# A gated cross-attention and feed-forward block on one core: the first layer of the feed-forward stage as seven half-sized block products

## The reference

```python
x = x + tanh(g_xattn) * attention(layernorm(x), ctx, ctx, w_q, w_k, w_v)   # causal, 8 x 1024 rows of 512
h = gelu(einsum('bsd,fd->bsf', layernorm(x), ternary(W1)) + b1)             # 512 -> 2048, exact gelu
x = x + tanh(g_ffn) * (einsum('bsf,df->bsd', h, ternary(W2)) + b2)          # 2048 -> 512
```

## Time and profile before

| | |
|---|---|
| median of 3 runs | 1661.05 us |
| profiled execution, own time | 1659.3 us |
| its span | 1657.5 us |
| TensorE busy (8492 products) | 1625.6 us, 98% |
| VectorE, ScalarE, GpSimd busy | 54%, 39%, 19% |
| TensorE clock granted, mean | 0.994 |
| feed-forward stage: its first second-layer product | at 769.41 us |
| one group of 512 rows in that stage | (1652.5 - 823.1) / 15 = 55.3 us |

### The profile page before, as it was taken

One profiled execution on the slowest core, in us unless ns is written; L12 is line 12 of the kernel. 1 busy time (PEld: TensorE's weight loads), 2 busy tenths in 40 slices (PEclk: granted clock), 3 DMA queues, 4 the chain that ended last, 5 costly groups with the idle time before them and its releaser, 6 DMA issues.

```text
span 1657.5 us, 23707 instructions
## 1 busy us (share of the span) xinstructions
PE 1625.6 (98%) x8492; PEld 830.7 (50%) x8492; DVE 889.5 (54%) x1595; ACT 652.3 (39%) x1032; POOL 311.5 (19%) x337
## 2 busy tenths in 40 slices
PE   7899999999999999999999999999999999999998
PEld 4455655565655565554444444444444444444444
DVE  6656666575666568884344344434443444344432
ACT  2333333333243345333443444434443544344443
POOL 3211111111111111131122112211221122122200
PEclk9899999999999999999999999999999999999999
DMA  6446455545545489953122212221222022202210
GB/s 203 113 97 148 103 143 106 139 106 132 120 98 148 92 237 224 214 139 102 44 52 70 63 36 59 70 63 26 69 70 63 19 76 70 63 19 76 70 32 26
DMA packets 261398, 157.50 MB, mean 95 GB/s; under 512 B 222080, under 2 KB 222096, under 8 KB 260048
## 3 DMA queue, kind: packets, MB, share of 16 engines
q1 hardware_dynamic: 260432, 154.21, 36.4%
q10 hardware_dynamic: 720, 2.10, 0.3%
q0 software_dynamic: 176, 0.27, 0.1%
HBM read 70.53 MB, written 33.55 MB: 63 GB/s over the span
## 4 chain that ended last, share of the span: by engine, by line
PE 89%; DVE 3%; issue 2%; DMA 1%; ACT 1%; SPq 0%; POOL 0%; DVEq 0%; ACTq 0%
PE s_ps L1090 12%; PE e_ps L1090 12%; PE s_ps L1016 11%; PE o_ps L1048 11%; PE t_ps L978 10%; PE v_ps L997 10%; PE o_ps L952 6%; PE t_ps L952 6%; PE v_ps L952 6%; PE m_ps L952 6%; DVE v_s L890 1%; DMA raw<-out_y 1%; DVE v_s L916 0%; ACT v_s L563 0%; ACT g L560 0%
## 5 line engine op out<-in xcount | busy, mean ns | idle before, releaser
L890 DVE SCALAR_TENSOR_TENSOR v_s<-g,sc,v_s 128x512 f16<-128x512 f32 x256 | 245.6, 969 | 382.4 <-ACT v_s L563 377.1
L1090 PE MATMUL s_ps<-w_s,v_s 128*128 128x512 f16 x1024 | 262.9, 379 | 6.2 <-DVE v_s L890 6.1
L1090 PE MATMUL e_ps<-w_s,v_s 128*128 128x512 f16 x1024 | 262.8, 379 | 0.0
L1016 PE MATMUL s_ps<-ctx_s,tT 128*128 128x512 f16 (+3 forms) x1152 | 199.3, 328 | 2.3 <-DVE tT L727 2.3
L1048 PE MATMUL o_ps<-v_s,pT 128*128 128x512 f16 x840 | 191.6, 379 | 0.0
L481 ACT ACTIVATE p<-s_ps,ebias,esc 128x128 f32<-128x128 f32 (+3 forms) x64 | 53.2, 831 | 351.3 <-DVE ebias L769 351.3
L563 ACT ACTIVATE v_s<-g,sc 128x512 f16<-128x512 f32 x256 | 184.8, 722 | 8.4
L978 PE MATMUL t_ps<-xnT,a_s 128*128 128x256 f16 x1488 | 175.9, 276 | 8.8 <-issue 8.7
L997 PE MATMUL v_ps<-wv_s,ctx_s 128*128 128x512 f16 x768 | 177.9, 382 | 2.8 <-DVE v_s L734 2.8
L1090 PEld LDWEIGHTS s_ps<-w_s,v_s 128*128 128x128 f16 x1024 | 98.9, 98 | 130.4 <-DVE v_s L890 10.8
L978 PEld LDWEIGHTS t_ps<-xnT,a_s 128*128 128x128 f16 x1488 | 146.0, 99 | 33.4 <-issue 10.4
(11 more groups left out here) (127 smaller groups left out, 1599.6 us busy)
## 6 DMA issues: line engine op xcount, KB each, us to landing
x_ring<-in_x SPq DMA_DIRECT2D x64, 256.0 KB, 2.9
out_y<-x_ring SPq DMA_DIRECT2D x64, 256.0 KB, 2.1
raw<-out_y SPq DMA_DIRECT2D x64, 256.0 KB, 3.1
out_y<-v_s SPq DMA_DIRECT2D x64, 256.0 KB, 2.1
raw<-in_ctxT SPq DMA_DIRECT2D x7, 2048.0 KB, 8.7
w_in<-in_w1T SPq DMA_DIRECT2D x16, 512.0 KB, 4.2
w_in<-in_w2T SPq DMA_DIRECT2D x16, 512.0 KB, 4.9
raw<-in_ctxT SPq DMA_DIRECT2D x2, 1024.0 KB, 16.8
```

Source lines behind the costliest of these rows:

```text
L890: v.scalar_tensor_tensor(out=g_s[:, f % 4, LO], in0=g32[:, f % 2], scalar=col(C_SG), in1=g_s[:, f % 4, HI], op0=ALU.mult, op1=ALU.subtract ...
L1016: last_mm = mm(s_ps[:, lo:hi], tT[:, pr, ta, c, q * P:(q + 1) * P], ctx_s[:, par, ca, c, lo:hi], start=(n == 0 and c == 0), stop=(n == 2 a ...
L1090: last_mm = mm(y_ps[i], g_s[:, f % 4, a, i * P:(i + 1) * P], w2_s[:, f, :], start=(f == 0 and a == HI), stop=(f == FC - 1 and a == LO))
```

## The change

Each group's first layer is written as 2 x 2 blocks: the 512 rows in two halves of 256, the inner dimension in two halves of 256, the hidden units in pairs of 128. Seven block products (Strassen's scheme in the form with 15 additions) take the place of eight. A unit `U` is 4 blocks `f` of one group, so there are 64 units. In each unit:

- TensorE: `unit_product` 1 to 7, each 8 products of 128 weights x 256 rows (56 instead of 32 products of 512), in four pieces (`unit_first`, `_second`, `_third`, `_last`) that alternate with the four blocks of the second layer (`back`) of the unit before.
- Three PSUM banks are copied out by ScalarE (R1, R2, R3) and one by VectorE (R5); two sums are made on VectorE and one on GpSimd (`last_sum`); gelu runs on 8 pieces of 256 columns, six of them from SBUF.
- The normalized rows are made in pairs of tiles (`y_stats`, `y_scale`, `y_normal`): four sums of 256 columns on GpSimd (`y_sums`), then one upper-half pass of 1792 columns on ScalarE (`y_upper`), one lower-half pass of 1792 columns on GpSimd (`y_lower`), and one DMA transpose of 3584 columns (`turn_y`). There are two pairs to a group.
- Weight sums: four sums of 1024 columns on GpSimd and four on VectorE, once, in the last slots of the attention stage.
- The feed-forward loops are written out; before, they were loops of the sequencers.

```diff
+            def turn_y(q):
+                sp.wait_ge(y_lo, q + 1)
+                dst = yT[q // 2 % 2].rearrange("p a o c n -> p (a o c) n")[:, :, q % 2 * P:(q % 2 + 1) * P]
+                sp.dma_start_transpose(dst, rows_at(q)[1].rearrange("p a o n -> p (a o n)")).then_inc(y_turned, 16)
...
+            def y_sums(q):
+                r8 = rows_at(q)[0]
+                pool.wait_ge(y_rows, 2 * q + 2)
+                g.tensor_tensor(r8[:, 4], r8[:, 0], r8[:, 2], ALU.subtract).then_inc(y_comb, 1)
+                g.tensor_tensor(r8[:, 6], r8[:, 1], r8[:, 0], ALU.subtract).then_inc(y_comb, 1)
+                pool.wait_ge(y_comb, 4 * q + 1)
+                g.tensor_tensor(r8[:, 5], r8[:, 1], r8[:, 4], ALU.subtract).then_inc(y_comb, 1)
+                pool.wait_ge(y_comb, 4 * q + 3)
+                g.tensor_tensor(r8[:, 7], r8[:, 3], r8[:, 5], ALU.subtract).then_inc(y_comb, 1)
...
+            def y_lower(q):
+                r8, r7 = rows_at(q)
+                pool.wait_ge(y_hi, q + 1)
+                g.tensor_tensor(r7[:, LO].rearrange("p o n -> p (o n)"), r8[:, 1:8].rearrange("p o n -> p (o n)"),
+                                r7[:, HI].rearrange("p o n -> p (o n)"), ALU.subtract).then_inc(y_lo, 1)
...
+            def weight_sums():
+                pool.wait_ge(w_ternary, NW // 2)
+                pool.wait_ge(t_mm, NT)
+                for c in range(2):
+                    g.tensor_tensor(wS[0][:, c], w1v[:, 0, c, :, 1], w1v[:, 1, c, :, 1], ALU.add).then_inc(w1_sums, 1)
+                for c in range(2):
+                    pool.wait_ge(w1_sums, c + 1)
+                    g.tensor_tensor(wS[1][:, c], wS[0][:, c], w1v[:, 0, c, :, 0], ALU.subtract).then_inc(w1_sums, 1)
...
+            def last_sum(U):
+                pool.wait_ge(r5_out, U + 1)
+                pool.wait_ge(r3_out, U + 1)
+                g.tensor_tensor(rr[:, R3], rr[:, R3], rr[:, R5], ALU.add).then_inc(c22_sum, 1)
...
+            last_sum(0)
+            for U in range(NU):
+                G = U // UG + 1
+                if U % UG == 0 and G < NG:
+                    y_scale(G * GT)
+                    y_scale(G * GT + 1)
+                if U % UG == 1 and G < NG:
+                    y_scale(G * GT + 2)
+                    y_scale(G * GT + 3)
+                    y_lower(2 * G)
+                    y_sums(2 * G + 1)
+                if U % UG == 2 and G < NG:
+                    y_lower(2 * G + 1)
+                    for e in range(GT):
+                        add_bias(G * GT + e)
+                if U + 1 < NU:
+                    last_sum(U + 1)
+                if U % UG == 0 and G < NG:
+                    y_sums(2 * G)
...
+            def unit_top(U, rows_q=None, rows_q_late=None):
+                act.wait_ge(h_mm[1], U + 1)
+                a.activation(rr[:, R1], bank_a[U % 2], ACT.Copy).then_inc(r1_out, 1)
+                if rows_q is not None:
+                    y_upper(rows_q)
+                act.wait_ge(c11_sum, U + 1)
+                if U:
+                    act.wait_ge(g_split, 4 * U - 2)
+                for p in range(2):
+                    gelu(U, p, 2 * p, 0, halves(rr[:, R1], p))
+                act.wait_ge(h_mm[6], U + 1)
+                a.activation(rr[:, R2], bank_a[U % 2], ACT.Copy).then_inc(r2_out, 1)
+                act.wait_ge(c12_sum, U + 1)
+                for p in range(2):
+                    gelu(U, 2 + p, 2 * p, 1, halves(rr[:, R2], p))
+                upper(U, 0, 3)
+                act.wait_ge(h_mm[7], U + 1)
+                a.activation(rr[:, R3], bank_a[U % 2], ACT.Copy).then_inc(r3_out, 1)
+                upper(U, 1, 4)
+                if rows_q_late is not None:
+                    y_upper(rows_q_late)
+            def unit_end(U):
+                act.wait_ge(c22_sum, U + 1)
+                if U:
+                    act.wait_ge(g_split, 4 * U)
+                for p in range(2):
+                    gelu(U, 4 + p, 2 * p + 1, 1, halves(rr[:, R3], p))
+                act.wait_ge(h_mm[4], U + 1)
+                for p in range(2):
+                    gelu(U, 6 + p, 2 * p + 1, 0, halves(bank_a[U % 2], p))
+                act.wait_ge(g_act, 8 * U + 8)
+                act.sem_inc(c21_read, 1)
+                upper(U, 2, 7)
+                upper(U, 3, 8)
...
+            def y_normal(e):
+                r, u = e % 2, e // GT % 2 * GT + TILE[e % GT]
+                slots = (2, 4) if r == 0 else (0, 2)
+                dst = rows_at(e // 2)[0][:, slots[0]:slots[1]].rearrange("p o n -> p (o n)")
+                dve.wait_ge(y_rstd, e + 1)
+                if e >= 2:
+                    dve.wait_ge(y_lo, e // 2)
+                v.tensor_scalar(dst, x2_in[:, u], mv[:, r, 0:1], rstd[:, r:r + 1], ALU.subtract,
+                                ALU.mult).then_inc(y_rows, 1)
...
+            def unit_first(U):
+                dve.wait_ge(h_mm[5], U + 1)
+                if U:
+                    dve.wait_ge(c22_sum, U)
+                v.tensor_copy(rr[:, R5], bank_c).then_inc(r5_out, 1)
+                dve.wait_ge(h_mm[2], U + 1)
+                dve.wait_ge(r1_out, U + 1)
+                v.tensor_tensor(rr[:, R1], rr[:, R1], bank_b, ALU.add).then_inc(c11_sum, 1)
+            def unit_second(U):
+                dve.wait_ge(h_mm[3], U + 1)
+                dve.wait_ge(r2_out, U + 1)
+                v.tensor_tensor(rr[:, R2], rr[:, R2], bank_c, ALU.add).then_inc(c12_sum, 1)
...
+            lower(0, 0)
+            lower(0, 1)
+            for U in range(NU):
+                G = U // UG + 1
+                if U and U % UG == 0:
+                    finish_rows(U // UG - 1)
+                if U + 1 < NU:
+                    unit_first(U + 1)
+                lower(U, 2)
+                lower(U, 3)
+                if U % UG == 1 and G < NG:
+                    for e in (G * GT + 2, G * GT + 3):
+                        y_stats(e)
+                    for e in (G * GT + 2, G * GT + 3):
+                        y_normal(e)
+                if U + 1 < NU:
+                    unit_second(U + 1)
+                    lower(U + 1, 0)
+                    lower(U + 1, 1)
+                if U % UG == 0 and G < NG:
+                    for e in (G * GT, G * GT + 1):
+                        y_stats(e)
+                    for e in (G * GT, G * GT + 1):
+                        y_normal(e)
+            finish_rows(NG - 1)
...
+            def unit_product(U, k, first):
+                g, bank = U // UG, (bank_a[U % 2], bank_b, bank_c)[(0, 0, 1, 2, 0, 2, 0, 0)[k]]
+                row = (None, B11, B21, B22, T4, T1, T2, T3)[k]
+                for p in range(2):
+                    m = U % UG * 2 + p
+                    for a in (HI, LO):
+                        for c in range(2):
+                            w = (None, w1v[:, 0, c, m, 0], w1v[:, 1, c, m, 0], wS[3][:, c, m], w1v[:, 1, c, m, 1],
+                                 wS[0][:, c, m], wS[1][:, c, m], wS[2][:, c, m])[k]
+                            last_mm = mm(bank[:, p * 2 * P:(p + 1) * 2 * P], w, yT[g % 2][:, a, row, c, :],
+                                         start=(first and p == 0 and a == HI and c == 0),
+                                         stop=(a == LO and c == 1), skip_group_check=True)
+                last_mm.then_inc(h_mm[k], 1)
...
+            def unit_first(U):
+                if U % UG == 0:
+                    pe.wait_ge(y_turned, 16 * (2 * (U // UG) + 2))
+                if U >= 2:
+                    pe.wait_ge(c21_read, U - 1)
+                if U == 1:
+                    pe.wait_ge(o_done, NT - 1 + O0)
+                unit_product(U, 1, True)
+                if U:
+                    pe.wait_ge(c12_sum, U)
+                unit_product(U, 5, True)
+                if U:
+                    pe.wait_ge(c11_sum, U)
+                unit_product(U, 2, True)
+            def unit_second(U):
+                pe.wait_ge(r1_out, U + 1)
+                unit_product(U, 6, False)
+                if U == 0:
+                    pe.wait_ge(w1_sums, 5)
+                pe.wait_ge(r5_out, U + 1)
+                unit_product(U, 3, False)
+            def unit_third(U):
+                pe.wait_ge(r2_out, U + 1)
+                unit_product(U, 7, False)
+            def unit_last(U):
+                pe.wait_ge(r3_out, U + 1)
+                unit_product(U, 4, False)
...
-                    pe.wait_ge(w_ternary, NW // 2)
-                    hidden(0, 0, 0)
-                    hidden(1, 1, 0)
-                    hidden(2, 2, 0)
-                    pe.wait_ge(o_done, NT - 1 + O0)
-                    hidden(3, 3, 0)
+                    pe.wait_ge(w1_sums, 4)
+                    unit_first(0)
...
+            unit_last(0)
             pe.wait_ge(w_ternary, NW)
-
-            def group(it, gg, last=False):
-                g = it * 2 + gg
-                for f in range(FC):
-                    F = g * FC + f
-                    pe.wait_ge(g_split, F + 1)
```

(31 more changed lines are left out.)

281 lines of the change are left out of this document (151 added, 130 removed).

## The result

The changed kernel took **1755.5 us** (median of 4 runs, 1754.6 to 1757.4) against 1660.4 us (4 runs, 1659.6 to 1661.9) before: a ratio of 1.058, 95% interval 1.056 to 1.059. It is 5.8% slower. The forecast was 1759 us: 98 us more than before, where 95.1 were measured.

A forecast was written before the change was run, and what follows sets the result against it. TensorE was taken to bound the kernel nearly throughout. Span 1657.5 - 50.8 (products) + 138 (crossings) + 15.5 (entry) - 4.3 (old waits) = 1755.9 us, giving a forecast time of 1759 us; range 1705 to 1806.

The forecast's parts named there:

- The products: First-layer products on TensorE: half-width ones at 0.109 us each, 442.2 us down to 391.4, saving 50.8 us.
- old waits: TensorE's earlier waits for VectorE in the feed-forward stage, replaced by the new ones: 4.3 us less.
- Product 4's wait: At each of 15 crossings TensorE waits 6.4 us for ScalarE's R3 copy, behind a serial chain through GpSimd's `y_lower`.
- Product 6's wait: At each crossing TensorE waits 1.1 us for the R1 copy, since GpSimd's `last_sum` stands behind two roots.
- The clock: TensorE's clock falls after each long crossing wait, losing 1.7 us each time; 0 as the other end.
- The crossing in sum: Making the next group's rows, 15 times: 6.4 + 1.1 + 1.7 us each, 138 us in all.
- The entry: Entry of the feed-forward stage: GpSimd's list delays the first transposed rows, costing 15.5 us (10 to 22).
- mutual holding: At the stage's entry GpSimd and VectorE hold each other up, about three times, 3 us.
- Rival 1: Row preparation at the crossings stays hidden, so the kernel gets faster, about 1620 us; chance 0.08.
- Rival 2: Slower still, about 1806 us: ScalarE waits for a transpose of 10 us or more, or engines block mutually; chance 0.20.
- Rival 3: Half the wait at crossings: no clock loss, short passes, 3 to 4 us each, 1690 to 1715 us; chance 0.07.
- Rival 4: Half-sized first-layer products save nothing, as each brings its own weight load: 1810 us; chance 0.01.

The follow-up runs named there:

- Run 3: Changed kernel with GpSimd's lower-half pass of groups 1 to 15 cut to 256 of its 1,792 columns (work left out): 1704.8 us, ratio 1.027.
- run 4: Changed kernel with VectorE's two normals of the second pair moved behind the next unit's sum and two lower halves: 1765.0 us, ratio 1.064.
- run 8: Changed kernel with GpSimd's last sum ahead of the two roots, and ahead of the biases in other units: 1729.0 us, ratio 1.043.
- run 9: Changed kernel with separate buffers for the second pair of rows, all orders as they were: 1755.6 us, ratio 1.059.
- run 2: Changed kernel with 24 further unused TensorE products ahead of product 4's wait in each of 15 crossing units: 1744.2 us, ratio 1.051.
- run 10: run 9 with 20 further unused TensorE products ahead of product 4's wait in the 15 crossing units: 1715.3 us, ratio 1.034.
- Run 5: Changed kernel with only the stage's entry edited: GpSimd's four weight sums moved to VectorE, its bias behind row sums and lower halves: 1746.9 us, ratio 1.053.

## Why the prediction was right

The sign, the mechanism and the time were right. Some of the agreement is errors that cancel: the entry was put 3.4 us too high and the saving 2.5 too low, the crossings 3.6 too low.

- **The products**: right in price (0.109 us). Term and old waits together gave 57.6, not 55.1. The old waits were under-read: the blocks behind them start 6.0 us late in all, where the rows list 4.3 (behind 778.04 the next block starts 2.88 us later in place of 1.73, and the row below says 1.00). The last 0.8 us I leave open.

```profile
778.04 1.89 PE L952 MATMUL m_ps<-ctx_s,w_s 128*128 128x512 f16 x8
780.92 1.04 PE L1090 MATMUL s_ps<-w_s,v_s 128*128 128x512 f16 x4 [1.00 <-DVE v_s L890]
```

- **Product 4's wait**: right in place, releaser and cause, 5.79 us instead of 6.4. `y_lower` took 3.58 us (forecast 3.8), a gelu piece 0.50 (forecast 0.5). Run 3 shows the pass in series, run 4 VectorE's order.
- **Product 6's wait**: 1.13 us, forecast 1.1, from GpSimd's roots (run 8).
- **The clock**: right in kind, but mis-sized. I took the 1.7 us lost behind a wait of 2.80 for a wait of twice the length; it was 2.1 on average. The length of the wait alone does not give it: behind 2.88 us it is 1.4 to 2.9 (run 3), behind 4.7 us 1.3 to 2.8 (run 8), behind 5.2 us 2.4 to 2.7 (run 9), behind 5.79 us 1.8 to 2.45. The Trainium skill's rule (TensorE: Matmul & The Clock Gate, HAM oscillation) holds: all 15 crossings paid, and runs 2 and 10 ended it by giving TensorE work. Its return to full speed is not simply worth its loss: in run 2 most of it became other waits.
- **The crossing in sum**: 9.4 us, forecast 9.2. That is luck in part: the long wait came 0.6 us shorter and the clock 0.4 us dearer than forecast, and 0.4 us are in pieces that the forecast did not count.
- **The entry**: 12.1 us, with 15.5 forecast: the first product 12.9 late and 2.4 of low clock behind it, less 3.2 that the old entry lost. The first product came at 767.00 (forecast by the chain 766.4, with 3 us of mutual holding on top of it 769.4). The chain's start was 1.0 us earlier than taken; the four weight sums and the bias took 12.0 us, not 10.1, because GpSimd and VectorE held each other up there: the one weight sum with no VectorE instruction ahead of it took 2.12 us, as forecast (2.2), the others 2.3 to 3.0, and the bias 2.24 in place of 1.27. So the holding was real, 2 us of the 3. Run 5 gave 8.6 back.
- **Rival 1** (hidden, 1620) had the right number for a kernel whose orders allow it: 1614.8 and 1616.7 us. **Rival 2**: ScalarE did wait for the first pair's transposes, 2.3 us on average and 3.5 once, but under its cover, as the forecast had it; but for one wait of 0.4 us it counted only in runs 2 and 4. **Rivals 3 and 4** are out.
